# K weights of the first stage moved early, two x tiles added on DVE, statistics and the own tile on GpSimd

## What is computed

```python
def _layernorm(x, axis=-1, eps=1e-5):
    m = jnp.mean(x, axis=axis, keepdims=True)
    v = jnp.var(x, axis=axis, keepdims=True)
    return (x - m) / jnp.sqrt(v + eps)

def _L0_attn_a_ref(x, Wq, Wk, Wv):
    Q = jnp.einsum('bti,id->btd', x, Wq)
    K = jnp.einsum('bti,id->btd', x, Wk)
    V = jnp.einsum('bti,id->btd', x, Wv)
    m = jnp.einsum('btd,bt->td', K, V.sum(axis=-1))
    # scan over t: s = gamma * s + m[t]
    ...
    S = S.reshape(-1, T).T
    return S[None, :, :] * Q

x = x + _L0_attn_a_ref(_layernorm(x), Wq, Wk, Wv)      # B = 8, T = 2048, D = 1024
x = x + _L0_ffn_ref(_layernorm(x), w_router, W1, b1, W2, b2)
...
```

## Time and profile before

| what | value |
|---|---|
| median of 3 runs | 1960.49 us (1955.18 to 1962.06) |
| the profiled execution | 1966.91 us |
| its span, slowest core (core 4) | 1965.3 us |
| spans of the eight cores | 1940.0 to 1965.3 us |
| PE busy | 1659.0 us, 84% |
| DVE busy | 886.8 us, 45% |
| ACT busy | 705.6 us, 36% |
| POOL busy | 205.8 us, 10% |
| DMA | 201.15 MB, mean 102 GB/s |

### The profile page before, as it was taken

How to read it: one execution, slowest core, us unless ns; L and a number is a source line. 1 busy time by engine, 2 the same in 40 slices (tenths; PEclk the granted TensorE clock), 3 DMA queues, 4 the chain that set the end, 5 groups by cost and what they waited for, 6 DMA issues and landing times.

```text
span 1965.3 us, 23417 instructions; the slowest of 8 cores (1940.0 to 1965.3 us)
## 1 busy us (share of the span) xinstructions
PE 1659.0 (84%) x8118; PEld 791.0 (40%) x8266; DVE 886.8 (45%) x1699; ACT 705.6 (36%) x1066; POOL 205.8 (10%) x256
## 2 busy tenths in 40 slices
PE   2899997832799996898998999999999994289997
PEld 1444443311344443444544444444444442144443
DVE  4799995776122226256433332542222446511222
ACT  4899995238211134301333221430011101622112
POOL 2222221112010013000000000000000000300002
PEclk9999999875899997898999999999999997599999
DMA  8976762590166659800001010680054222173445
GB/s 240 284 238 230 256 232 54 102 192 33 55 103 109 111 133 215 188 1 1 33 12 37 8 43 1 129 139 1 1 87 85 43 44 54 43 244 60 82 86 86
DMA packets 69458, 201.15 MB, mean 102 GB/s; under 512 B 4644, under 2 KB 4708, under 8 KB 69344
## 3 DMA queue, kind: packets, MB, share of 16 engines
q0 software_dynamic: 40960, 94.76, 27.6%
q1 hardware_dynamic: 28384, 104.89, 16.0%
HBM read 228.97 MB, written 33.59 MB: 134 GB/s over the span
## 4 chain that ended last, share of the span: by engine, by line
PE 66%; ACT 10%; DMA 7%; DVE 6%; issue 5%; ACTq 3%; DVEq 1%; SPq 0%; POOL 0%; POOLq 0%
PE v_h1ps L1008 11%; PE v_h2ps L1020 10%; PE mlp_a L1694 6%; PE ab_bank L1529 5%; PE mlp_a L1682 5%; ACT scr_s L432 4%; ACT scr_s L427 3%; PE ab_bank L1567 3%; PE mlp_a L1708 3%; PE ab_bank L1473 3%; PE ab_bank L1423 3%; PE mlp_r L1708 3%; PE ab_big L1454 3%; PE ab_bank L1480 3%; PE ab_bank L1542 2%
## 5 line engine op out<-in xcount | busy, mean ns | idle before, releaser
L513 PE MATMUL yps<-ring,diag 128*128 128x512 f32 x448 | 204.0, 608 | 29.7 <-POOL diag L393 29.7
L1020 PE MATMUL v_h2ps<-m_w,m_h1q 128*128 128x512 bf16 x1000 | 221.1, 379 | 1.3
L1008 PE MATMUL v_h1ps<-m_sel_fm,m_w 128*128 128x512 bf16 x1006 | 221.0, 379 | 0.9
L957 ACT ACTIVATE m_h1q<-v_h1ps,fb_s 128x512 bf16<-128x512 f32 x128 | 87.8, 688 | 294.3 <-PE v_h1ps L1008 294.3
L933 DVE TENSOR_TENSOR m_acc<-v_h2ps,m_acc 128x512 f32<-128x512 f32 x96 | 66.3, 692 | 263.0 <-PE v_h2ps L1020 263.0
L590 DVE SCALAR_TENSOR_TENSOR scr_v<-ring,wvs_bc 128x1024 bf16<-128x1024 f32 x128 | 153.4, 1217 | 0.6 <-DMA ring<-x_all 0.3
L1020 PEld LDWEIGHTS v_h2ps<-m_w,m_h1q 128*128 128x128 bf16 x1024 | 100.2, 98 | 120.8
L1008 PEld LDWEIGHTS v_h1ps<-m_sel_fm,m_w 128*128 128x128 bf16 x1024 | 100.1, 98 | 120.4
L1666 ACT ACTIVATE gate_prod<-mlp_a 128x512 bf16<-128x512 f32 x64 | 38.2, 598 | 272.2 <-PE mlp_a L1682 272.0
L513 PEld LDWEIGHTS yps<-ring,diag 128*128 128x128 f32 x448 | 84.5, 194 | 127.3 <-issue 127.3
L1682 PE MATMUL mlp_a<-xln_fm,wg_buf 128*128 128x512 bf16 x502 | 111.6, 379 | 3.1 <-ACT gate_prod L1666 2.6
(11 more groups left out here) (263 smaller groups left out, 2257.2 us busy)
## 6 DMA issues: line engine op xcount, KB each, us to landing
ring<-x_all SPq DMA_DIRECT2D x64, 1024.0 KB, 7.3
m_w<-fW POOLq DMA_DIRECT2D x16, 2048.0 KB, 15.4
x_tok<-x_all POOLq DMA_DIRECT2D x16, 512.0 KB, 7.7
y_dram<-x_tok SPq DMA_DIRECT2D x4, 2048.0 KB, 23.6
x_tok<-y_dram SPq DMA_DIRECT2D x16, 512.0 KB, 4.3
x_tok<-y_dram POOLq DMA_DIRECT2D x16, 512.0 KB, 5.3
out<-x_tok SPq DMA_DIRECT2D x4, 2048.0 KB, 21.7
m_sel_tok<-sel_dram SPq DMA_DIRECT2D x8, 514.0 KB, 5.9
```

What stands on the lines that cost most here:

```text
L513: ii = t.matmul(yps[tt % 2][:, h * 512:(h + 1) * 512], lhsT=diag_of(n), rhs=x_tile(n)[:, h * 512:(h + 1) * 512], start=(n % B == 0), stop= ...
L957: s.activation(out=h1q[:, ft * D + h * 512:ft * D + (h + 1) * 512], in_=h1ps[n % 4][:, :], func=AF.Gelu_apprx_tanh, bias=fb1_s[:, q * 8 + ...
L1008: ii = t.matmul(h1ps[n % 4][:, :], lhsT=w1[:, dt * D + ft * P:dt * D + (ft + 1) * P], rhs=sel_fm[:, dt * D + h * 512:dt * D + (h + 1) * 51 ...
L1020: ii = t.matmul(h2ps[m % 4][:, :], lhsT=h1q[:, ff * D + rt * P:ff * D + (rt + 1) * P], rhs=w2[:, ff * D + h * 512:ff * D + (h + 1) * 512], ...
```

## The change

Four things, in the first 450 us:

1. **K weights.** `wk16` moves from the place of `wq16` (32 KiB) to 64 KiB, into old ring slots. POOL issues its load inside the loop, behind the diagonals of group 30, after waits for `a_ymm` of tile 14 and `a_z` 15. PE splits column 0: three quarters need `y_fm` of 15 tiles, the last needs all 16. `s_fm` moves to 32 KiB.
2. **x of the last two tiles.** SP loads the own x of tiles 7 and 15 into `x_last` (48 KiB) at the end of the loop; DVE adds them to the products of column 7. POOL's accumulating DMAs are 14 instead of 16. The statistics of tile 15 are taken by DVE (bn_stats), ACT does 15 tiles. Column 7's DVE order is scan, products, additions, dots of column 6, bn_stats, dots of column 7.
3. **FFN weights.** W1 and W2 are issued together after the second addition (`a_xsum` 2); W1 overlaps `x_last` in SBUF.
4. **POOL in the loop.** `roots` on POOL: variance + eps, then a `pow` with -1 for `inv8` (four columns) and, in even groups, a `pow` with -0.5 for `orst` (one column). The diagonal takes two scalars, `dotw` and `inv8`, so it doesn't need `coef`. `own_norm` is one POOL tensor_scalar (subtract the mean, times `orst`) of 128 x 1024 behind the diagonals of an even group. `mean_term` is six small POOL operations behind those of an odd group, the last one signals `a_nb`. DVE's `coefs` and `mean_term` and ACT's `own_norm` are gone; DVE's `y_finish` waits for `a_nb`, ACT's `z_scale` for `a_coef` from `mean_term`.

The core of the diff:

```diff
             for gi in range(NGRP):
-                g.wait_ge(sem('a_coef'), at('a_coef', gi + 1))
+                roots(gi)
                 for j in range(4):
...
-                    g.tensor_scalar(out=diag_of(n), in0=cS['ident32'][:, :], scalar1=coef[:, n:n + 1], scalar2=1.0,
+                    g.tensor_scalar(out=diag_of(n), in0=cS['ident32'][:, :], scalar1=dotw[:, n:n + 1], scalar2=inv8[:, n:n + 1],
                                     op0=ALU.mult, op1=ALU.mult).then_inc(sem('a_diag'), 1)
-            g.wait_ge(sem('a_qmm'), at('a_qmm', NT))
-            g.dma_start(out=wk16[:, :].rearrange('p (k n) -> p k n', k=ND),
-                        in_=wD['aWk'].rearrange('(k p) n -> p k n', p=P)).then_inc(sem('a_wk'), 16)
+                if gi == NGRP - 2:
+                    g.wait_ge(sem('a_ymm'), at('a_ymm', ymm_no(4 * (NT - 2) + 3)))
+                    g.wait_ge(sem('a_z'), at('a_z', NT - 1))
+                    g.dma_start(out=wk16[:, :].rearrange('p (k n) -> p k n', k=ND),
+                                in_=wD['aWk'].rearrange('(k p) n -> p k n', p=P)).then_inc(sem('a_wk'), 16)
+                if gi % 2 == 0:
+                    own_norm(gi // 2)
+                else:
+                    mean_term(gi // 2)
```

New on POOL:

```diff
+            def roots(gi):
+                c0, tt = 4 * gi, gi // 2
+                g.wait_ge(sem('a_dots'), at('a_dots', gi + 1))
+                g.wait_ge(sem('a_stat'), at('a_stat', gi + 1))
+                g.tensor_scalar(out=inv4[:, 0:4], in0=mv[:, 2 * c0 + 1:2 * c0 + 8:2], scalar1=1e-05, scalar2=None, op0=ALU.add)
+                g.drain()
+                g.tensor_tensor(out=inv8[:, c0:c0 + 4], in0=inv4[:, 0:4], in1=powers[:, 0:4], op=ALU.pow)
+                if gi % 2 == 0:
+                    g.tensor_tensor(out=orst[:, tt:tt + 1], in0=inv4[:, 0:1], in1=powers[:, 4:5], op=ALU.pow)
+                g.drain()
+
+            def own_norm(tt):
+                if tt >= 1:
+                    g.wait_ge(sem('a_owntr'), at('a_owntr', tt))
+                g.drain()
+                g.tensor_scalar(out=ownln[:, :], in0=x_tile(B * tt), scalar1=mv[:, 2 * B * tt:2 * B * tt + 1], scalar2=orst[:, tt:tt + 1],
+                                op0=ALU.subtract, op1=ALU.mult).then_inc(sem('a_ownln'), 1)
...
+                g.tensor_tensor(out=aw8[:, 0:B], in0=coef[:, c0:c0 + B], in1=cS['mean_scale'][:, :], op=ALU.mult)
+                g.drain()
+                g.tensor_tensor(out=aw8[:, B:2 * B], in0=mv[:, 2 * c0:2 * c0 + 16:2], in1=aw8[:, 0:B], op=ALU.mult)
...
+                g.tensor_tensor(out=nbias[:, tt:tt + 1], in0=aw8[:, 4:5], in1=aw8[:, 5:6], op=ALU.add).then_inc(sem('a_nb'), 1)
```

On POOL, SP and DVE behind the loop:

```diff
-            for i in range(NT):
+            for i in range(NT - 2):
...
-                if i == 7:
...
-                if i == 11:
...
+            g.wait_ge(sem('a_xsum'), at('a_xsum', 2))
+            g.dma_start(out=mod_buf[0]['w1'][:, :].rearrange('p (k n) -> p k n', k=ND),
...
+            for side in range(2):
+                tt = ND - 1 + side * (NT // 2)
+                s.dma_start(out=x_last[:, side * D:(side + 1) * D], in_=x_all[0, tt * P:(tt + 1) * P, :]).then_inc(sem('a_xlast'), 16)
...
+            v.wait_ge(sem('a_xlast'), at('a_xlast', 32))
+            v.drain()
+            for side in range(2):
+                tt = ND - 1 + side * (NT // 2)
+                v.tensor_tensor(out=x_tok[:, tt * D:(tt + 1) * D], in0=x_tok[:, tt * D:(tt + 1) * D],
+                                in1=x_last[:, side * D:(side + 1) * D], op=ALU.add).then_inc(sem('a_xsum'), 1)
+            v.drain()
+            router_dot(NT - 4)
+            router_dot(NT - 3)
+            bn_tile_hook(v, NT - 1)
+            router_dot_tile(v, 0, ND - 1, NT - 2)
+            router_dot_tile(v, 0, NT - 1, NT - 1)
```

More of the change, by code:

```diff
@@ L87 @@
     [('a_z', 16)],
+    [('a_dots', 32)],
+    [('a_nb', 16)],
     [('a_ysum', 16), ('ab_invA', 24)],
@@ L95 @@
     [('a_xadd1', 64), ('ab_wo_ld', 16), ('ab_wg1', 16)],
-    [('a_xadd2', 64), ('ab_wq_ld', 16), ('ab_wu1', 16)],
-    [('a_xadd3', 64)],
-    [('a_tstat', 16), ('ab_tev0', 36)],
+    [('a_xadd2', 48), ('ab_wq_ld', 16), ('ab_wu1', 16)],
+    [('a_xadd3', 48)],
+    [('a_xlast', 32)],
+    [('a_xsum', 2)],
+    [('a_tstat', 15), ('ab_tev0', 36)],
     [('ab_tmm1', 40)],
@@ L481, in attn_a_scalar @@
             q_evict(NT - 1)
-            for i in range(NT):
+            for i in range(NT - 1):
                 c, side = divmod(i, 2)
                 tt = c + side * (NT // 2)
-                s.wait_ge(sem(f'a_xadd{i % 4}'), at(f'a_xadd{i % 4}', 16 * (i // 4 + 1)))
+                if i == NT - 2:
+                    s.wait_ge(sem('a_xsum'), at('a_xsum', 1))
+                else:
+                    s.wait_ge(sem(f'a_xadd{i % 4}'), at(f'a_xadd{i % 4}', 16 * (i // 4 + 1)))
                 if i == 0:
@@ L529, in own_project @@
                     t.wait_ge(sem('a_wq'), at('a_wq', 16))
-                    t.wait_ge(sem('a_coef'), at('a_coef', 1))
+                    t.wait_ge(sem('a_dots'), at('a_dots', 1))
                 else:
@@ L558, in attn_a_tensor, with k_products @@
             own_transpose(NT - 1)
-            own_project(NT - 1)
-            y_transpose(NT - 1)
-            t.wait_ge(sem('a_yev'), at('a_yev', NT))
-            t.wait_ge(sem('a_qev'), at('a_qev', NT))
-            t.wait_ge(sem('a_wk'), at('a_wk', 16))
-            for c in range(ND):
-                if c >= 2:
-                    t.wait_ge(sem('a_scan'), at('a_scan', c - 1))
-                for nq in range(4):
+            def k_products(c, nqs):
+                for nq in nqs:
                     for dt in range(ND):
@@ L571, in attn_a_tensor @@
                                       start=(dt == 0), stop=(dt == ND - 1))
-                ii.then_inc(sem('a_mmm'), 1)
+                return ii
+            own_project(NT - 1)
+            y_transpose(NT - 1)
+            t.wait_ge(sem('a_wk'), at('a_wk', 16))
+            t.wait_ge(sem('a_yev'), at('a_yev', NT - 1))
+            k_products(0, (0, 1, 2))
+            t.wait_ge(sem('a_yev'), at('a_yev', NT))
+            k_products(0, (3,)).then_inc(sem('a_mmm'), 1)
+            t.wait_ge(sem('a_qev'), at('a_qev', NT))
+            for c in range(1, ND):
+                if c >= 2:
+                    t.wait_ge(sem('a_scan'), at('a_scan', c - 1))
+                k_products(c, range(4)).then_inc(sem('a_mmm'), 1)
         @blk.vector
@@ L629, in y_finish @@
                 v.wait_ge(sem('a_z'), at('a_z', tt + 1))
+                v.wait_ge(sem('a_nb'), at('a_nb', tt + 1))
                 if tt >= 1:
                     v.wait_ge(sem('a_ytr'), at('a_ytr', tt))
-                v.drain()
                 for h in range(2):
@@ L658, in attn_a_vector @@
                 tiles(2 * tt)
-                coefs(2 * tt)
                 if tt >= 2:
@@ L691, in attn_a_vector @@
                                     in1=sc[:, side::2], op=ALU.mult).then_inc(sem('a_prod'), 1)
-                if c >= 1:
+                if 1 <= c < ND - 1:
                     router_dot(2 * c - 2)
                     router_dot(2 * c - 1)
-            router_dot(NT - 2)
-            router_dot(NT - 1)
+            v.wait_ge(sem('a_xlast'), at('a_xlast', 32))
[10 more added lines that the diff above has]
+            router_dot_tile(v, 0, NT - 1, NT - 1)
+            v.bn_aggr(ag2[:, 2 * NT - 2:2 * NT], bn12[:, 12 * (NT - 1):12 * NT])
+            v.drain()
+            v.tensor_scalar(out=ag2[:, 2 * NT - 2:2 * NT - 1], in0=ag2[:, 2 * NT - 2:2 * NT - 1], scalar1=1.0 / 32.0, scalar2=None, op0=ALU.mult)
     def bn_tile_hook(v, tt):
```

71 lines of the change are left out of this document (26 added, 45 removed).

## The result

The changed kernel took 1976.0 us, median of seven runs (1972.6 to 1982.9); the kernel before took 1960.9 beside it (median of six, 1955.2 to 1965.6). Some executions of every kernel run slower at a lower clock on one half of the chip; they are left out of all times here. The ratio is 1.0084 [1.006, 1.0107]: slower by 0.8%, where 1921 us and 2% faster had been forecast. The profiled execution took 1975.25 us, its span 1973.6 (core 6; rows of before are of core 4, span 1965.3).

What follows compares the result with a forecast made beforehand. ACT was taken to pace the first loop at 17.72 us a tile, DVE the part behind it. Gains of 14.8 (loop), 16.5 (K weights), 4.9 (FFN weights) and 3.0 (x), 39.2 us, took 1960.5 to 1921, range 1911 to 1946.

Steps and rivals of the forecast that it cites:

- Drains at 0.1: 1.0.: First loop, POOL: about 10 drains a tile at 0.1 us each, 1.0 us in all.
- What is queued behind POOL's new waits ... Cost nothing.: Loop end, POOL: own tile 15, roots and diagonals 31 stand behind the K issue; claimed to cost nothing.
- The cover of 10.8 us: Loop end: PE's even group, projections and transposes, 10.8 us of work before it wants what POOL has queued.
- POOL's own work: First loop: POOL's instructions and drains per tile, 8.9 us, bounds 6.6 and 14.0, before blocking.
- The blocking: First loop: POOL waiting out DVE's dots, 4.9 us a tile, half of at most 9.8; POOL then needs 13.8.
- Rival (d): First loop: POOL paces above 17.72 us a tile; 1936 to 1960 us; chance 0.10.
- PE's floor: First loop: PE's own instructions need 16.49 us a tile, so at most 1.23 of ACT's 2.05 us are gained.
- K weights early: Behind the first loop: the wait for K weights goes and the scan starts 16.5 us earlier, bounds 14 and 18.
- FFN weights and x on DVE: K columns up to the router step: 4.9 us from later FFN weights, 3.0 from the last two tiles' x on DVE.
- rival (c): K weights land late or FFN loads hit the scatters: up to 9 us back, 1930 us; chance 0.05.
- The rule on the lock: SBUF: a two-input DVE instruction and a POOL instruction reading SBUF exclude one another for a whole instruction.
- Rival (b): First loop: DVE or POOL paces at 16.6 to 17.72 us a tile, own tile stopping a dot; 1927 to 1936; chance 0.17.

Runs made afterwards that it cites:

- e1_sem: The changed kernel with POOL's drains in the first loop replaced by waits on POOL's own semaphore; 1950.5 and 1946.8 us in two executions.
- e9_onedrain: e1_sem with one POOL drain put back, ahead of own tile 15, behind the issue of the K weights; ratio to the kernel before 1.0008.
- e6_nopow: e1_sem with POOL's `pow` replaced by a multiplication of the same shape, leaving out reciprocals and root; ratio to the kernel before 0.9767.
- e7_dvemean: e1_sem with the coefficients' product and the mean term moved back from POOL to DVE; 1924.3 us, ratio to the kernel before 0.9813.
- e2_drain: The kernel before with one POOL drain added behind the first group's diagonals; ratio to the kernel before 1.0032.
- e3_nopool: The changed kernel without its POOL part: coefficients and mean term on DVE, own tile on ACT, as before; 1936.8 us, ratio to the kernel before 0.9847.
- e8_half: e1_sem with the own tile's normalization on POOL over 512 of its 1024 columns, the rest zero; ratio to the kernel before 0.9866.

## Why the prediction was wrong, point by point

**"Drains at 0.1: 1.0."** This step failed, and it carries the sign. I costed ten drains as gaps and didn't ask what a drain waits for. Nearly all are cheap (0.1 to 0.24 us); of the whole loop the two that follow an issue of POOL took 23.43 and 15.20 us. The earlier trace rows held the K issue and its 16.9 us to the first product, no row had the Wq issue (at 30.75 in the trace of before), and none a drain on POOL, so no row of before could show the price. I should have bounded it by the load's own length, as for any other operation without a row. A rival "a new drain holds POOL until its load lands, 17 us at the seam" would have ended at 1921 + 17 = 1938, and with the 16 us that the early one cost, near 1954. By the medians of the marks the drains cost 30.9 us (after against e1_sem).

**"What is queued behind POOL's new waits ... Cost nothing."** I listed the own tile, the roots and the diagonals 31 behind the K issue, and asked only whether the issue itself came late. The cover of 10.8 us was for the issue; the queue behind needed the load's 16.0. It cost 37.26 - 21.12 = 16.1 us: 13.41 of waiting and 2.5 for the odd group that follows, 7.93 us in place of 5.39. e9_onedrain shows it alone, by 15.35 us. Without the drain the cover was enough: in e1_sem the odd group starts at 330.21, right behind the transposes and without a wait.

**POOL's own work.** This is the second step that failed. The middle was 8.9 us with bounds of 6.6 to 14.0. It is 12.8: own tile 3.78 (1.7 taken, bound 2.9), three `pow` 2.63 (1.5), seven diagonals 3.07 (2.5), eight small ones 1.66 (2.2), gaps 1.69 (1.0). The own tile is the term that fell outside its bounds: 8 diagonals were taken as dear enough for 1024 columns. The blocking was right in sum, 18.06 - 12.8 = 5.2 against 4.9 taken; half of the most it could be was a guess, so that is luck. Together 18.06 instead of 13.8, above PE's 16.49 and above the old 17.72. The sign of being wrong that the prediction names, POOL busy throughout and a wait for diagonals in each group, is there. Rival (d) had this, with a chance of 0.10 and 1936 to 1960; e1_sem, which is the change without the stalls, landed there with 1947 to 1951 (about 1943 if held against its kernel before). e6_nopow and e7_dvemean show the cause: with either cut, 2.0 us of `pow` or the mean part (3.7 us of busy time), PE's floor is back. By the medians of the marks, this step cost 8.2 + 14.8 = 23.0 us of the loop: e1_sem is 8.2 later than before, 14.8 earlier had been forecast.

**The early stall isn't absorbed.** Not in the prediction at all. In e2_drain 13 of 19 us came back: part never reached PE's tile 1, and the steady loop's 17.72 left 1.2 us a tile to a PE that could do 16.49. With POOL at 18.06 nothing came back: 16.4 us behind e1_sem at tile 1, 16.0 at tile 15.

**PE's floor, ACT and DVE.** Right: 16.49 forecast, 16.47 measured in e7_dvemean; ACT 15.67 and 15.63. DVE's 15.3 was without a mean term: it is busy for 15.60 of 18.06 us in the changed kernel, with 0.9 us lost to blocking on two dots, and for 15.56 in e7_dvemean, where the mean term is back at 0.9.

**K weights early.** Right: from the last transposes to the first scan it is 8.7 us now and was 26.4; 17.7 gained, 16.5 forecast, within 14 to 18. The scan follows the router row, as said; in e3_nopool the last thing it waits for is PE's first column, by 0.34 us.

**FFN weights and x on DVE.** Right: from first scan to router step 80.55 us, was 89.18; 8.6 gained, 7.9 forecast. The columns run at 9.53, and L889 comes 9.27 us after the products' end (461.87 - 452.60), 9.3 forecast. The later FFN weights cost nothing, as said: the first scatter starts 24.9 us behind the router step (24.3 before), the first FFN matmul 63.5 (64.7 before). So rival (c) didn't occur.

**Sum.** Forecast -14.8 - 16.5 - 7.9 = -39.2. Ledger +41.0 - 17.7 - 8.6 = +14.7. The 54 us between lie in the loop and its end: 30.9 by the drains and 23.0 by POOL's period (medians of the marks). Without the stalls and with a POOL short enough (e7_dvemean) the change gives 1.87% of 1961, 36.7 us, and the interval [26 to 47] holds the forecast's 39.2. Its last transposes are 14.2 us earlier than before (330.8 - 316.6), 14.8 forecast.

**The rule on the lock.** The prediction weighed the Trainium skill (SBUF — State Buffer, Who interferes with whom): exclusion for a whole instruction. The trace bears out half. Small operations of POOL do wait out a dot (2.07 us in place of 1.04, 1.02 in place of 0.20). A long one doesn't hold DVE off for its length: the own tile runs from 210.26 to 215.87, and in it DVE does this:

```profile
209.73 1.41 DVE L636 SCALAR_TENSOR_TENSOR scr_v<-ring,wvs_bc 128x1024 bf16<-128x1024 f32 x1
...
211.07 1.21 DVE L636 SCALAR_TENSOR_TENSOR scr_v<-ring,wvs_bc 128x1024 bf16<-128x1024 f32 x1
...
212.45 1.89 DVE L636 SCALAR_TENSOR_TENSOR scr_v<-ring,wvs_bc 128x1024 bf16<-128x1024 f32 x1 [0.16 <-issue]
```

POOL needs 3.78 us unblocked and took 5.61, DVE lost 0.2 and 0.7 us on two dots. Nearly all of the 4.1 us from 210.26 to 214.34 is a dot, and POOL lost only 1.8: both went forward side by side. Rival (b)'s price, a dot stopped for the whole own tile, didn't occur.

## What to carry to other kernels

A drain on POOL isn't a gap: cost it by the longest transfer that POOL has issued and that is still under way, and wait for the one result that is needed by a semaphore. (No drain of another engine behind its own transfer was measured here.) When an engine takes over work, sum its whole new period, each term bounded by what its rows can't exclude, before counting what the relieved engine gives back: 2 us of POOL's 18 decided between a loop at 18.1 and one at 16.5 (e6_nopow), while 1.7 us less of another instruction gave only 0.7 (e8_half). A stall early in the loop was paid in full where the engine that stalled also paced it (the changed kernel), and by a third where it didn't (e2_drain).

## What the runs showed of the hardware

- A POOL drain waits for POOL's own transfers: 23.43 us (Wq landing after 32.8), 15.20 (K, 16.0), 19.38 in e2_drain (Wq, 30.7), 15.35 in e9_onedrain (K, 15.5). Transfers of other queues don't count: in the steady loop, with SP's x loads under way (DMA share 0.64), the gaps at drains are 0.1 to 0.24 us. POOL goes on 0.2 to 0.8 us behind the landing in all four; whether the drain waits for the data or for something else of the transfer that ends with it isn't told apart. The wait is the drain's alone: in e1_sem POOL works on at full speed right behind the same issues (own tile 3.80 us at 323.53).
- `pow` on POOL takes 1.04 us for four columns and 0.55 for one; a multiplication of the same shape 0.20.
- A normalization of 1024 columns from f32 to bf16 takes POOL 3.78 us and ACT 1.24; 512 columns take 2.09, so 3.3 ns a column. The Trainium skill (GPSIMD Engine Reference, Performance versus the Vector engine) led to an estimate of 0.9 to 1.5 us plus dispatch; the measurement decides against it.
- The wait of 13.4 us costs PE's clock too. PE does next to nothing from 346.3 on; the granted clock is 1.00 (2.4 GHz) up to 350, 0.50 (1.2 GHz) from 355 to 363, and 1.00 again from 365, with PE at work since 359.75. The group behind the wait takes 7.93 us in place of 5.39. (Windows of PE before, in and after the wait; 0.69 and 0.67 are means over both levels.)

```profile
335.33:345.70 10.37, 10.31 (x31) 4.59 (x33) 3.33 (x6) 2.95 (x6) 3.19 (x4) 1.00 0.48 73
346.20:359.70 13.50, 0.14 (x3) 0.00 (x0) 0.69 (x1) 0.00 (x0) 5.59 (x5) 0.69 0.52 92
359.75:367.50 7.75, 7.75 (x12) 3.21 (x13) 0.00 (x0) 2.12 (x3) 1.89 (x8) 0.67 0.00 0
```
